# VectorE's sums of the running states in front of the low half of the normed output, in every attention step

## The reference

```
q, k, v = h @ Wq, h @ Wk, h @ Wv            # 8 heads of 128, chunks of 128 tokens
for each chunk:
    attn = where(causal, q k^T, 0)
    o = attn @ v + q @ S                     # S: running state of the head, 128 x 128
    S = S + k^T v
y = sum over heads of rmsnorm(o) * w @ Wo
```

## Time and profile before

| | us |
|---|---|
| median of three runs | 1061.51 |
| the profiled execution, its own time | 1064.03 |
| its span in the profile | 1062.3 |
| TensorE busy with matmuls / weight loads | 1051.6 / 960.8 |
| VectorE busy | 891.8 |
| ScalarE busy | 558.5 |

### The profile page before, as it was taken

One profiled execution on the slowest core, in us unless ns is written; L12 is line 12 of the kernel. 1 busy time (PEld: TensorE's weight loads), 2 busy tenths in 40 slices (PEclk: granted clock), 3 DMA queues, 4 the chain that ended last, 5 costly groups with the idle time before them and its releaser, 6 DMA issues.

```text
span 1062.3 us, 18981 instructions
## 1 busy us (share of the span) xinstructions
PE 1051.6 (99%) x6790; PEld 960.8 (90%) x6790; DVE 891.8 (84%) x1860; ACT 558.5 (53%) x1604; POOL 47.3 (4%) x68
## 2 busy tenths in 40 slices
PE   9999999999999999999999999999999999999998
PEld 6899999989989999998999889999999999999997
DVE  6788888888877888888777898888888888888887
ACT  6765765756656657657565634443333333333332
POOL 1000000000000000000000000101001010101010
PEclk9999999999999999999999999999999999999999
DMA  6555355455363553654445622253323233323213
GB/s 218 163 171 168 109 173 169 137 157 167 135 191 115 173 179 120 188 171 128 162 149 185 175 73 91 81 159 100 115 90 120 85 120 99 120 85 96 83 59 112
DMA packets 166222, 143.10 MB, mean 135 GB/s; under 512 B 28784, under 2 KB 162928, under 8 KB 166128
## 3 DMA queue, kind: packets, MB, share of 16 engines
q1 hardware_dynamic: 165440, 141.88, 42.9%
q10 hardware_dynamic: 688, 0.00, 0.0%
HBM read 77.27 MB, written 64.57 MB: 134 GB/s over the span
## 4 chain that ended last, share of the span: by engine, by line
PE 88%; DMA 5%; DVE 3%; ACT 2%; SPq 1%; issue 1%; POOL 0%; DVEq 0%; ACTq 0%; POOLq 0%
PE ps L263 69%; PE ps L724 4%; PE ps L776 4%; PE ps L770 4%; PE ps L754 4%; DMA moved<-work 2%; DMA r_gate<-moved 2%; SPq L417 1%; PE ps L859 1%; PE ps L652 1%; PE ps L612 0%; DVE work L1404 0%; DVE work L1521 0%; ACT work L947 0%; ACT work L994 0%
## 5 line engine op out<-in xcount | busy, mean ns | idle before, releaser
L263 PE MATMUL ps<-r_k,r_gate_up 128*128 128x512 f32 x768 | 185.2, 391 | 0.7 <-DVE r_k L1587 0.7
L263 PEld LDWEIGHTS ps<-r_k,r_gate_up 128*128 128x128 f32 x768 | 141.5, 188 | 28.1 <-issue 0.9
L263 PE MATMUL ps<-r_o,onT 128*128 128x256 f32 x768 | 106.8, 288 | 0.0
L263 PE MATMUL ps<-r_h,r_k 128*128 128x512 f32 (+1 forms) x393 | 105.2, 403 | 0.0
L263 PEld LDWEIGHTS ps<-r_q,r_v 128*128 128x128 f32 x768 | 99.7, 191 | 4.9 <-DVE r_v L1655 0.3
L263 PE MATMUL ps<-r_q,r_v 128*128 128x256 f32 x768 | 102.3, 283 | 0.0
L967 ACT ACTIVATE work<-ps 128x128 f32<-128x128 f32 x256 | 67.3, 278 | 59.4 <-PE ps L776 59.1
L263 PE MATMUL ps<-r_h,r_q 128*128 128x512 f32 x384 | 98.2, 391 | 0.0
L263 PE MATMUL ps<-r_v,r_h 128*128 128x512 f32 x384 | 97.4, 390 | 0.0
L263 PEld LDWEIGHTS ps<-r_o,onT 128*128 128x128 f32 x768 | 95.8, 190 | 0.1
L1162 ACT ACTIVATE r_v<-work 128x512 fp32r<-128x512 f32 x64 | 40.5, 633 | 99.2 <-DVE work L1651 99.1
(11 more groups left out here) (161 smaller groups left out, 2054.2 us busy)
## 6 DMA issues: line engine op xcount, KB each, us to landing
moved<-work SPq DMA_DIRECT2D x63, 512.0 KB, 2.9
r_gate<-moved SPq DMA_DIRECT2D x252, 128.0 KB, 2.5
kept_h<-work SPq DMA_DIRECT2D x31, 384.0 KB, 2.6
work<-kept_h SPq DMA_DIRECT2D x124, 96.0 KB, 2.2
work<-in_L_attn_hidden_states SPq DMA_DIRECT2D x15, 512.0 KB, 5.3
kept<-work SPq DMA_DIRECT2D x9, 514.0 KB, 4.4
kept_h<-work SPq DMA_DIRECT2D x9, 512.0 KB, 3.4
kept_xq<-work SPq DMA_DIRECT2D x8, 512.0 KB, 5.6
```

Of the source, the lines that this page charges most:

```text
L263: done = pe.matmul(out_ap, a, b, start=first and n == 0, stop=last and n == 2, skip_group_check=skip)
```

## The change

In every step but the first two and the last, the low half of onT is made behind the three sums of the states, not ahead of them. Nothing else is changed: the same instructions with the same operands stand on every engine, and TensorE's, ScalarE's and SyncE's lists are the same.

```
                     early_extras(b, j, mine)
                     if final and j == STEPS - 1:
                         last_o_lo(t0 + j - 1)
-                    elif not first or j >= LAG:
-                        o_lo(t0 + j - 1)
                     dve.wait_ge(ds_done, t0 + j + 1)
                     last = carry[:, h, :] if s else None
                     for c in range(updates(j)):
...
                         last = to
+                    if (not first or j >= LAG) and not (final and j == STEPS - 1):
+                        o_lo(t0 + j - 1)
                     late_extras(b, j, mine)
```

## The result

The changed kernel takes 1082.28 us (median of four runs, 1081.48 to 1082.92), the kernel before 1061.12 beside it (1060.58 to 1062.41). The ratio is 1.0194, with a 95% interval of 1.0181 to 1.0207: slower by some 21 us, where I had forecast 15 (1076.5, range 1069 to 1085). The sign and the mechanism were right, the size was too small. A second set of runs of the same kernel gave 1081.48 against 1062.69 (23 runs of before, 1060.03 to 1064.78), a ratio of 1.0173 (1.0158 to 1.0189), so part of the first 21 us may have been the draw of four runs: the two intervals overlap at 1.0181 to 1.0189, about 19 to 20 us.

The account below looks back on a forecast made before the run. TensorE was taken to bound the kernel, busy 99% of the span. The terms 12.4 + 1.8 + 0.2 + 0.4 + 2.1 - 1.9 summed to 15.0 us, on a median of 1061.51 giving 1076.5 us, range 1069 to 1085.

Parts of the forecast that it names:

- TensorE bounds, so only its standstill counts: Whole kernel: TensorE is busy 99% of the span; VectorE's order costs or gains only where TensorE comes to wait.
- The new chain, first half on time, 18 x 0.69: First-half steps, first state on time: projection's load waits behind shares, first state, three sums, low half; 12.4 us.
- The low half starts 0.08 early and takes 0.65: VectorE behind the third sum: low half starts 0.08 us before the sums end, takes 0.65 us, not 0.69.
- Second-half steps, 23 x 0.09 = 2.1: Second-half steps without transposes or a standstill for a sum: projection's load comes 0.09 us later each, 2.1 us.
- Five standstills, -1.9: Five second-half steps: TensorE's 2.4 us standstill for sums goes, 5 x 0.09 comes in its place, -1.9 us.
- +0.1 each: Two first-half steps with VectorE late: sums start earlier, the pair ends when it did; 2 x 0.1 = 0.2 us.
- First state late, 6 x 0.3: Six first-half steps with ScalarE late: ScalarE gets ahead of TensorE, cost between 0.1 and 0.68 each; 1.8 us.
- The term that I put at nothing: VectorE's late extras start 0.57 us later, norm and exchange up to 0.1 late in such a step; costed at nothing.
- The median: Forecast 1079.0 from the profiled execution, lowered by 2.52 to the median of the runs shown: 1076.5 us.
- The faster one: Rival 1: sums come sooner, projection never waits for the low half; 3.5 us go, 1058.0 us; chance 0.04.
- The one of waits given back elsewhere: Rival 3: new standstill replaces TensorE's waits for the turned k and unseen lateness; +8, 1069.4 us; chance 0.11.
- The signs: Profile after: line 1304 releases TensorE's loads some 50 times, 15 to 17 us; growing line 1404 waits would refute it.

Follow-up runs that it names:

- the run with two sums: Changed kernel with the low half behind two of the three sums in all steps: 1077.19 us, ratio 1.0134 to the kernel before.
- the low products last: Changed kernel with the output projection's 8 high-half products first, then the 4 that read the low half: 1065.35 us, ratio 1.0021 to the kernel before.

## Why the prediction was right, and where it was too small

- *TensorE bounds, so only its standstill counts.* Right: VectorE's busy time did not grow, and the 17.45 us are in the attention steps but for 0.4.
- *The new chain, first half on time, 18 x 0.69.* Right in mechanism and nearly in size: 0.72 a step. Shown by the order of the starts, by the run with two sums (0.32 less a step) and by the low products last (the standstill gone).
- *The low half starts 0.08 early and takes 0.65.* The start was right, the length 0.68: a middle value between the two rows that I had weighed.
- *Second-half steps, 23 x 0.09 = 2.1.* The term that was most mis-sized: 3.5 us, 0.15 a step. Of the 0.06 too little, 0.03 is the length of 0.68. The rest is a second semaphore, which I left out: the wait for `dve1_done` moves from the low half to the first sum in about half of the steps and delays its start by 0.07, and at h = 2 TensorE's load has two waits and starts 0.06 later.
- *Five standstills, -1.9.* I misread. The 2.4 us are not all in the second half. Two of the five are the first-half steps with VectorE late, and they hold 1.51 us of it (the other is at 502.15, with 0.79):

```profile
218.24 0.62 PEld L776 LDWEIGHTS ps<-work 128*128 128x128 f32 x4 [0.72 <-DVE work L1557]
```

  So I counted their standstill in the wrong half and gave the steps themselves +0.1 each. Measured, these two lost 0.5 us less than before. The second half did have five steps with a late third sum, three in the rows and two with standstills too short for one, and they gave back 1.2. That both counts were five is luck.
- *First state late, 6 x 0.3.* I took it that ScalarE gets ahead of TensorE. At h = 1 it hardly did:

```profile
183.28 0.63 ACT L957 ACTIVATE onT<-work 128x512 fp32r<-128x512 f32 x1 [1.27 <-DVE work L1521]
183.40 1.05 PE L754 MATMUL ps<-work 128*128 128x128 f32 x8
...
184.77 0.28 ACT L989 ACTIVATE work<-ps 128x128 f32<-128x128 f32 x1
```

  ScalarE waits for the turned output and copies the first state 0.32 behind the shares' end (184.45); before it was 0.44 (shares from 178.59 to 179.64), on time it is 0.04. So 0.12 was caught up, and these three steps lost 0.6 each, nearly the full price. The term that I put at nothing is VectorE's lost slack. I had read the slack (0.51 us) from a step with h = 4, and not from h = 0, whose extras are those that delay the next step. That lost slack at h = 0 costs the next step 0.6 is shown with the low products last; for the changed kernel itself it is argued from the same step length. The three other steps differ by -0.9, +0.4 and +1.1. Two of them differ as much between the two traces of one kernel (10.36 and 12.06 us, 10.59 and 9.91), so these sizes hang on the execution that was traced.
- *The median.* I took the forecast down to a median of three runs that most later sets put 1.1 to 1.3 us higher. From the profiled execution, 1079.0 was forecast and 1081.48 measured.
- *The rivals.* The faster one fell: its point of decision, a low half that ends by the load's start, was missed by 0.7 us in each first-half step with the first state on time. The one of waits given back elsewhere holds in small part: the loads' waits for the turned k went from 3.7 us to 2.2, and single late steps gave time back, but far from 8 us. The clock stayed full.
- *The signs.* I had looked for some 50 entries of line 1304, two thirds of them in the first half, with 15 to 17 us; there are 23 entries with 14.3 us, all in the first half. The low half took 0.68, not 0.65. The waits for line 1404 fell, and from the last scores to the end the two traces differ by 0.25 us, as good as nothing, as forecast.

What stays open: how much of the change's cost comes back as chance lateness that is absorbed (the traces say 17.45 us, the medians 19 to 21), and whether the lost slack alone makes up the late first states of the changed kernel.

## What to carry to other kernels

When an engine's work is reordered so that an urgent result comes first, look at what waits for the work that goes to the back, and count the chain from the last event that both hang on: a piece that was made in idle time for nothing becomes a serial link in every step. If the result is split, let the consumer start on the part that is there and wait for the rest as late as it can; that took away most of the cost here without touching the producer. The slack behind the moved piece is to be read in the step with the least of it, not in a typical one. And look at which waits move along with the piece: a wait that cost nothing off the path can land on it.

## What the runs showed of the hardware

- An instruction with more semaphores to wait for starts later behind the last of them. VectorE's first sum starts 0.11 us behind the shares' end with two and 0.04 us with one (13 and 14 starts in the trace after), 0.13 us behind ScalarE's copy with three and 0.10 us with two; TensorE's load starts 0.12 us behind the low half with two and 0.05 us with one. How long VectorE had been idle makes no difference: with one semaphore it is 0.04 us at every idle time from 0.15 to 2.2 us.
- GpSimd makes the low half of 128 x 512 in 1.31 us on average, against VectorE's 0.68, beside a busy VectorE, whose three sums still take 0.94:

```profile
L595 POOL TENSOR_TENSOR onT<-work,onT 128x512 fp32r<-128x512 f32 x61 | 79.9, 1309 | 484.9 <-ACT onT L961 484.9
```

I had reckoned 1.8, twice the 0.9 us that its 128 x 256 operations of the later stages take on average; these range from 0.73 to 1.38 us, so no rule for its time follows.
